# Gate scans in two halves of 64 rows, one of them amid the heads; weight rounding on GpSimd

## What is computed

```python
B, S, D, H = 16, 256, 256, 8
# x, ctx: (16, 256, 256)

def mlstm(q, k, v):                    # per batch; k = v = ctx
    ifg = jnp.concatenate([q, k, v], axis=-1)
    ig = (ifg @ igate_w.T + igate_b).T
    fg = (ifg @ fgate_w.T + fgate_b).T
    cs = jnp.cumsum(jax.nn.log_sigmoid(fg), axis=1)
    log_D = where(tril, cs[:, :, None] - cs[:, None, :], -inf) + ig[:, None, :]
    max_log_D = jnp.max(log_D, axis=-1, keepdims=True)
    C = einsum('hsd,htd->hst', qh, kh) / sqrt(32) * jnp.exp(log_D - max_log_D)
    norm = jnp.maximum(jnp.abs(C.sum(-1, keepdims=True)), jnp.exp(-max_log_D))
    h = einsum('hst,htd->hsd', C / (norm + EPS), vh)
    return layernorm(h) * ln_scale

def fake_quant_weight(w):              # 8 bits, one scale for the tensor
    scale = jnp.max(jnp.abs(w)) / 127
    return jnp.clip(jnp.round(w / scale), -128, 127) * scale

x = x + tanh(g_xattn[0]) * mlstm(layernorm(x), ctx, ctx)
x = x + tanh(g_ffn[0]) * lora_ffn(layernorm(x))     # both weights fake-quantised
x = x + tanh(g_xattn[1]) * attention(layernorm(x), ctx)
x = x + tanh(g_ffn[1]) * moe(layernorm(x))
return x
```

## Time and profile before

| | |
|---|---|
| median of three runs | 1244.83 us |
| the profiled execution | 1246.31 us, of which the span of its records 1244.7 us |
| TensorE busy | 1131.0 us (91%) |
| VectorE busy | 890.8 us (72%) |
| ScalarE busy | 699.2 us (56%) |
| GpSimd busy | 427.4 us (34%) |

### The profile page before, as it was taken

The page is one execution under the profiler, slowest core; times in us unless marked ns, Lnnn a source line. Parts: engine busy times, 40 slices in busy tenths (PEclk is TensorE's granted clock), DMA queues, the critical chain, the costliest instruction groups (busy, mean ns, idle before and its releaser), DMA issues. The chain is left out here.

```text
span 1244.7 us, 28091 instructions
## 1 busy us (share of the span) xinstructions
PE 1131.0 (91%) x9256; PEld 956.5 (77%) x9257; DVE 890.8 (72%) x2039; ACT 699.2 (56%) x1580; POOL 427.4 (34%) x559
## 2 busy tenths in 40 slices
PE   4958887999998799999999789889999999998997
PEld 1336565798987577777766489778999999997997
DVE  6739998667676788888887378457666767664656
ACT  1358875555563467676665544246655555553543
POOL 1237885713121110110130025664223333224563
PEclk9868989999998899999998978889999999998999
DMA  9245651100003564454452037658355454535564
GB/s 324 66 175 205 201 200 33 44 0 0 0 0 73 110 138 100 87 119 101 89 107 54 3 130 269 238 189 278 118 170 168 154 166 163 168 128 161 187 197 142
DMA packets 97181, 163.51 MB, mean 131 GB/s; under 512 B 12039, under 2 KB 71707, under 8 KB 94779
## 3 DMA queue, kind: packets, MB, share of 16 engines
q1 hardware_dynamic: 87067, 134.51, 37.2%
q0 software_dynamic: 9264, 27.01, 6.3%
q10 hardware_dynamic: 752, 0.73, 0.2%
HBM read 102.47 MB, written 33.69 MB: 109 GB/s over the span
## 5 line engine op out<-in xcount | busy, mean ns | idle before, releaser
L1677 DVE TENSOR_REDUCE c_mx<-c_s 128x2 f32<-128x512 f32 x256 | 164.4, 686 | 20.4 <-PE c_s L1823 20.1
L1598 ACT ACTIVATE c_probs<-c_t 128x512 f32<-128x512 f32 x256 | 139.0, 597 | 28.8 <-PE c_t L1846 27.9
L2773 ACT ACTIVATE d_g_full<-d_bank,d_e_bias 128x256 f32<-128x256 f32 x156 | 77.6, 497 | 108.6 <-PE d_bank L34 108.6
L32 PE MATMUL d_bank<-de_zt_hi,d_e_hi 128*128 128x256 f32 x312 | 91.1, 292 | 0.0
L34 PE MATMUL d_bank<-d_w_hi,d_g_lo 128*128 x312 | 88.0, 282 | 0.0
L33 PE MATMUL d_bank<-d_w_lo,d_g_hi 128*128 x312 | 88.0, 282 | 0.0
L34 PE MATMUL d_bank<-de_zt_hi,d_e_lo 128*128 128x256 f32 x312 | 87.8, 281 | 0.0
L32 PE MATMUL d_bank<-d_w_hi,d_g_hi 128*128 x312 | 87.8, 281 | 0.0
L33 PE MATMUL d_bank<-de_zt_lo,d_e_hi 128*128 128x256 f32 x312 | 87.6, 281 | 0.0
L2802 DVE TENSOR_TENSOR d_g_lo<-d_g_full,d_g_hi 128x256 fp32r<-128x256 f32 x156 | 65.9, 461 | 24.7 <-ACT d_g_hi L2774 24.7
L2933 POOL DMA_INDIRECT d_w_lo<-d_y_rows,d_pos x64 | 62.9, 983 | 56.4 <-ACT d_g_hi L2946 19.4
(11 more groups left out here) (413 smaller groups left out, 3814.2 us busy)
## 6 DMA issues: line engine op xcount, KB each, us to landing
d_e_raw<-in_w SPq DMA_DIRECT2D x39, 514.0 KB, 3.6
a_mb<-a_maxima SPq DMA_DIRECT2D x16, 1024.0 KB, 7.6
d_w_hi<-d_zt_kept SPq DMA_DIRECT2D x26, 512.0 KB
d_z_in<-d_z_rows POOLq DMA_DIRECT2D x39, 256.0 KB, 4.2
d_y_rows<-de_ys SPq DMA_DIRECT2D x39, 256.0 KB, 2.1
c_kt<-c_k_hi SPq DMA_DIRECT2D x64, 128.0 KB, 3.2
c_qt<-c_q_hi SPq DMA_DIRECT2D x64, 128.0 KB, 3.7
d_zt_kept<-d_w_hi SPq DMA_DIRECT2D x32, 256.0 KB
```

The source lines that it names most:

```text
L32: tensor.matmul(out, lhs_hi, rhs_hi, start=start, stop=False)
L1598: act.activation(probs[h % PR][:], t_ps[k][:], ACT.Exp).then_inc(exp_done, 1)
L1677: dve.tensor_reduce(mx[n % 2][:, :, k, p:p + 1], s_ps[h % SB][:], AX.X, ALU.max).then_inc(max_done, 1)
L2773: act.activation(g_full[:, m, :], hid[m][:, 0:TOK], ACT.Gelu, bias=bias[u][:, m:m + 1]).then_inc(gelu_full, 1)
```

## The change

The rows of gates are treated in two halves of 64 rows (batches 0 to 7 and 8 to 15), by a class `GateRows` whose tiles live on through the heads' stage.

- First half: in the gates' loop. `sizes(0)` is at VectorE's i = 6, Exp and Ln are on ScalarE behind step 5, `scans(0)` is at VectorE's i = 7 ahead of norm(7), the threshold on ScalarE behind step 6, and the transposes on TensorE ahead of query(7). SP stores its maxima behind the rows of step 6, and loads batch 0's once the rows of step 7 are issued.
- Second half: amid the heads. `sizes(1)` is in batch 0 and `scans(1)` in batch 1 on VectorE, each behind the first two products; Exp and Ln are on ScalarE behind the decays of batch 0, the threshold behind those of batch 1; the transposes are in batch 2 on TensorE, which then waits for VectorE's copy. SP stores its maxima ahead of its load of mb for batch 3.
- The two weights are rounded by GpSimd, one of the three passes behind each of `rstds(2)` to `rstds(7)`.
- In the heads' stage GpSimd's masks(0) stands ahead of the two memsets of va.

The diff, cut to its core:

```diff
+class GateRows:
+    HALVES = 2
+    LAST = 2
...
+        self.last_rows = sb("last_rows", [Mlstm.ROWS, self.LAST * S])
+        self.placed = [sem(f"placed{k}") for k in range(3)]
...
+    def wait_placed(self, engine, k):
+        steps = ((4,), (3, 1))[k]
+        for i, n in enumerate(steps):
+            engine.wait_ge(self.placed[k + i], 64 * n)
+    def sizes(self, dve, k):
+        self.wait_placed(dve, k)
+        f = self.part(self.f, k)
+        dve.scalar_tensor_tensor(out=self.part(self.size, k), in0=f, scalar=-1.0, in1=f, op0=ALU.mult, op1=ALU.max).then_inc(self.size_done, 1)
+    def logarithms(self, act, k):
+        small = self.part(self.small, k)
+        act.wait_ge(self.size_done, k + 1)
+        act.activation(small, self.part(self.size, k), ACT.Exp, scale=-1.0).then_inc(self.exp_done, 1)
+        act.wait_ge(self.exp_done, k + 1)
+        act.activation(small, small, ACT.Ln, bias=1.0).then_inc(self.ln_done, 1)
+    def scans(self, dve, k):
+        step = Chain(dve, self.scan, 2)
+        step.begin(k)
+        f, small, log_f = self.part(self.f, k), self.part(self.small, k), self.part(self.size, k)
+        cs, a, m = self.part(self.cs, k), self.part(self.a, k), self.part(self.m, k)
+        dve.wait_ge(self.ln_done, k + 1)
+        dve.wait_ge(self.zero_set, 1)
+        step(dve.scalar_tensor_tensor(out=log_f, in0=f, scalar=0.0, in1=small, op0=ALU.min, op1=ALU.subtract))
+        step(dve.tensor_tensor_scan(cs, log_f, self.part(self.zero, k), 0.0, ALU.add, ALU.add))
+        dve.tensor_tensor(a, self.part(self.gate_i, k), cs, ALU.subtract).then_inc(self.a_done, 1)
+        dve.wait_ge(self.a_done, k + 1)
+        dve.tensor_tensor_scan(m, a, a, -3e38, ALU.max, ALU.max).then_inc(self.m_done, 1)
+        dve.wait_ge(self.m_done, k + 1)
+        dve.scalar_tensor_tensor(out=small, in0=cs, scalar=-1.0, in1=m, op0=ALU.mult, op1=ALU.subtract).then_inc(self.max_done, 1)
+    def thresholds(self, act, k):
+        act.wait_ge(self.max_done, k + 1)
+        act.activation(self.part(self.thr, k), self.part(self.small, k), ACT.Exp).then_inc(self.thr_done, 1)
+    def turn(self, pe, k, out):
+        corner = self.ident[self.N * k:self.N * (k + 1), self.N * k:self.N * (k + 1)]
+        for i, (rows, done) in enumerate(((self.a, self.a_done), (self.thr, self.thr_done))):
+            pe.wait_ge(done, k + 1)
+            for j in range(Mlstm.J):
+                mm = pe.transpose(out[:, i, j, :], self.part(rows, k)[:, j * P:(j + 1) * P], corner)
+        mm.then_inc(self.turned, 1)
+    def keep_turned(self, dve, k, out):
+        dve.wait_ge(self.turned, k + 1)
+        dve.tensor_copy(self.tok_all[:, :, :, self.N * k:self.N * (k + 1)], out).then_inc(self.tok_done, 1)
+    def keep_maxima(self, sync, k):
+        b = Mlstm.B // self.HALVES
+        sync.wait_ge(self.m_done, k + 1)
+        sync.dma_start(self.m_dram[b * k:b * (k + 1)].rearrange("b h s -> (b h) s"), self.part(self.m, k)).then_inc(self.m_kept[k], 16)
...
+        SCANNED, PLACED = STEPS // 2, STEPS - 1
+        def gate_rows(n, some):
+            return g_rows[some, n * TOK:(n + 1) * TOK] if n < PLACED else rows.last_rows[some, :]
         def place_rows(queue, n, at, dst):
...
+            placed = rows.placed[0 if n < SCANNED else 1 if n < PLACED else 2]
+            for b in range(2):
+                row = H * (2 * n + b)
+                queue.dma_start(dst[row:row + H, :], gate_rows(n, slice(at, at + H))[:, b * S:(b + 1) * S]).then_inc(placed, 16)
...
+                place_rows(sync, n, 0, rows.f)
+                if n < PLACED:
+                    place_rows(sync, n, LO, rows.gate_i)
+                if n == STEPS - 2:
+                    rows.keep_maxima(sync, 0)
+            sync.wait_ge(rows.m_kept[0], 16)
             first.load_maxima(sync)
-            sync.wait_ge(m_kept, 16)
+            for k in range(2):
+                sync.wait_ge(rows.placed[k], 64 * (SCANNED, PLACED - SCANNED)[k])
...
+            def quantise(i, part):
+                flat = w_raw[i][:]
+                kept = lora.w1[:].rearrange("p a b -> p (a b)") if i == 0 else lora.w2[:, :, 0:D]
+                if part == 0:
+                    pool.wait_ge(inverted, i + 1)
+                    pool.tensor_scalar(flat, flat, inv[:, i:i + 1], ROUND, ALU.mult, ALU.add).then_inc(scaled_w, 1)
+                if part == 1:
+                    pool.wait_ge(scaled_w, i + 1)
+                    pool.tensor_scalar(flat, flat, -ROUND, QMAX, ALU.add, ALU.min).then_inc(bounded, 1)
+                if part == 2:
+                    pool.wait_ge(bounded, i + 1)
+                    pool.tensor_scalar(kept, flat if i == 0 else flat.rearrange("p (a b) -> p a b", a=lora.KF), -QMAX - 1.0, None,
+                                       ALU.max).then_inc(rounded, 1)
             for n in range(STEPS):
                 rstds(n)
-            pool.wait_ge(built, 3)
+                if 2 <= n < 5:
+                    quantise(0, n - 2)
+                if n >= 5:
+                    quantise(1, n - 5)
...
                 if n in (4, 6):
                     raise_hi(0 if n == 4 else 1)
+                if n == 5:
+                    rows.logarithms(act, 0)
+                if n == 6:
+                    rows.thresholds(act, 0)
             act.wait_ge(rows_done, STEPS)
-            place_rows(act, STEPS - 1, LO, gate_i)
...
+            place_rows(act, STEPS - 1, LO, rows.gate_i)
...
-            def quantise(i):
...
                     largest(0)
                 if i == 2:
                     scales(0)
-                    quantise(0)
                 if i == 3:
                     split_down()
                 if i == 4:
...
                 if i == 5:
                     scales(1)
                     scale_by_tanh()
+                if i == 6:
+                    rows.sizes(dve, 0)
+                if i == 7:
+                    rows.scans(dve, 0)
                 if i == STEPS:
-                    quantise(1)
                     raise_lo(0)
                     raise_lo(1)
...
+                    rows.keep_turned(dve, 0, tok_ps[:])
+            dve.wait_ge(rows.tok_done, 1)
...
                 if n in (1, 4):
                     turn_amax(0 if n == 1 else 1)
                 turn(n)
+            rows.turn(pe, 0, tok_ps)
             query_part(STEPS - 1)
...
+        tok_ps = hvt[0][:, S:2 * S].rearrange("p (k j r) -> p k j r", k=2, j=J)
...
                 u = n % R
                 after(sync, decay_done, 2 * (n + 1 - MR) * H)
+                if n == 3:
+                    rows.keep_maxima(sync, 1)
+                if n == B // 2:
+                    sync.wait_ge(rows.m_kept[1], 16)
                 sync.dma_start(mb[n % MR][:], m_dram[n].partition_broadcast(P)).then_inc(m_loaded[n % MR], 16)
...
+            masks(0)
             for i in range(R):
                 pool.memset(va[i][:], 0.0).then_inc(built, 1)
-            masks(0)
             pool.wait_ge(built, R)
...
             for n in range(B):
                 act.wait_ge(masked, 2 * (n + 1))
+                if n == B // 2:
+                    act.wait_ge(rows.tok_done, 2)
                 for h in range(H):
                     decays(n, h)
...
                         keep_outputs(n - 1, 3)
+                if n == 0:
+                    rows.logarithms(act, 1)
+                if n == 1:
+                    rows.thresholds(act, 1)
             for g in range(GROUPS):
...
             for n in range(B):
                 for h in range(0, QUAD, PAIR):
                     weigh(n, h)
+                if n == 0:
+                    rows.sizes(dve, 1)
+                if n == 1:
+                    rows.scans(dve, 1)
                 if n >= 2:
                     h_stat(n - 2)
...
                     h_norm(n - 2)
+                if n == 2:
+                    rows.keep_turned(dve, 1, tok_ps)
                 if n >= 1:
                     normalise(n - 1)
...
                 scores(n, 1)
                 if n > 0:
                     turn_outputs(n - 1)
+                if n == 2:
+                    rows.turn(pe, 1, tok_ps)
+                    pe.wait_ge(rows.tok_done, 2)
                 if n == 0:
                     pe.wait_ge(built, 2 * R)
```

84 lines of the change are left out of this document (27 added, 57 removed).

## The result

The changed kernel takes 1257.8 us (median of four runs, 1254.0 to 1259.1) beside 1244.2 us of the kernel before (median of four), a ratio of 1.0088 with a 95% interval of 1.0061 to 1.0115: 0.9% slower (the two medians themselves lie 1.1% apart, inside that interval). Forecast were 1239.4 us and faster, in a range of 1234 to 1246. The profiled execution took 1259.1 us and its records span 1257.3; before's span 1244.7. The loss is 12.6 us in this pair of traces, and it stands in two places: the gates' stage with its GpSimd passes, and the heads.

What follows compares the result with a forecast made beforehand. It saw TensorE's 4.58 us beat and stall in the gates' loop, a serial tail, and later heads bound by VectorE. Gain of 8.55 at the maxima load less 3.1 in the heads gave -5.45 us: 1239.4, range 1234 to 1246.

Steps and rivals of the forecast that it cites:

- The price of a GpSimd pass: Gates' loop: a rounding pass over 2048 columns on GpSimd takes 2.15 us, between bounds of 2.1 and 4.7.
- The collision: Gates' loop: VectorE operations with two SBUF inputs wait for GpSimd; split_down's subtraction takes back about 2 us, leaving 3.7.
- It hides under 3.2 us a pass: Gates' loop: GpSimd's rstd of 1.4 us plus a pass fits TensorE's beat of 4.58, up to about 3.2 a pass.
- Rival C: Gates' stage: GpSimd becomes the bound, maxima load at 40.6 + 6q for q us a pass, kernel slower; chance 0.10.
- what leaves VectorE: Gates' loop: without rounding, step 2 turns near 28.5 at full clock; about 5.8 us gained without the collision.
- the tail: Behind the gates' loop: query(7)'s end to the load of the maxima takes 2.05 us instead of 9.99.
- Its landing: Start of the heads: batch 0's maxima, loaded at 63.7, let the first mask start at 68.7 instead of 77.22.
- ScalarE's insertion in the heads: After batch 0's decays: Exp, load, Ln and load add 3.45 us on ScalarE.
- The heads: Heads' stage: the second half's work costs 3.1 us, 6.5 if the maxima land late, no less than 1.
- The maxima of batch 3: Heads: their load, alone in the queue, takes 5 us; masks of batch 3 come at 100.2 to 102.4.
- The sum: Whole kernel: -8.55 at the load of the maxima and +3.1 in the heads give -5.45 us.

Runs made afterwards that it cites:

- The probe: The kernel before plus fourteen GpSimd passes over 2048 columns behind the gates' stage, seven alone and seven beside VectorE operations; 1278.5 us including the added work.
- changed_again: The changed kernel itself, run again on a second chip beside the kernel before; ratio 1.0086 (1.0054 to 1.0118).
- two_fast_passes: The changed kernel with two GpSimd passes a weight (multiply-add, then add and multiply by 1.0), clip left out; 0.9965 of the kernel before.
- fast_passes_heads_reordered: The changed kernel with two fast GpSimd passes, second maxima's store moved to batch 6 and transposed half's copy ahead of h_norm; 0.9985 of the kernel before.
- two_fast_passes_scans_whole: The kernel before with rounding on GpSimd in two fast passes a weight, clip left out, scans whole behind the loop; ratio 0.9990 (0.9971 to 1.0009).

## Why the prediction was wrong

By the steps of the prediction:

- **The price of a GpSimd pass failed.** "A pass has one tensor input, like the cast: I take 2.15." The bounds were 2.1 and 4.7, and the passes took 1.98, 7.16, 5.38 and 1.98, 7.17, 5.80, which is 4.91 in the mean. The cast at 1.04 us for 1024 columns shares the one tensor input but not the pair of operations. No row of before had a tensor_scalar of that width on GpSimd; I bounded it by rows of other operations and then took the lower end, and the upper bound, for all its distance, lay below two of the three passes of each weight. The Trainium skill, "GPSIMD Engine Reference", section "Engine selection", calls one-input work there roughly line rate. The runs contradict that for five of the seven passes priced alone.
- **The collision failed, in whom it holds.** I counted only "a VectorE operation with two SBUF inputs". The probe has tensor_scalar and copy from SBUF held longer (5.02 and 4.95 us) than subtraction and scan (3.43 and 3.69). The norm, the cast, the copy and the small tensor_scalar of the loop were therefore not free; the subtraction of split_down, the one that I had named, ran free at 28.93 (0.21 us), and the cast behind it was held. The Trainium skill, "SBUF — State Buffer", section "Who interferes with whom", has copy, cast and tensor_scalar among those that can take the shared ports, and tensor_reduce not. The probe agrees on copy, tensor_scalar and tensor_reduce, the changed kernel's trace on the cast. I had used one half of that section, the half that my row showed. The section's words on a lock for the whole instruction, which the prediction puts to two inputs from SBUF, stand there with the two-port modes of the first three; that is also how the runs have it, since the operations with two inputs were let go 1.2 to 1.5 us before the pass ended.
- **"It hides under 3.2 us a pass" failed with them,** and not only by the size. It asked whether GpSimd has room in a beat of 4.58. It had: its rstd was never waited for. The other question, what stands still on VectorE while the pass runs, has the pass's whole length for an answer whenever VectorE comes to one held operation. Of the five holds, that of the cast made TensorE wait 6.62 us and that of the norm 3.76, and behind both it ran at half clock.
- **Rival C had the sign and the place, but too little.** Its formula, 40.6 + 6q, gives 70.1 at the measured mean of 4.91; the load was at 78.1. It put six passes and five rstds back to back. In the trace GpSimd stands idle 2.62, 0.74, 2.02 us for statistics that VectorE reached late, behind the held cast, copy and tensor_scalar: the engines took turns, and each one's delay came back to the other. Its chance of 0.10 rested on the row of the cast.
- **Right: what leaves VectorE.** Turn of step 2 at 28.5 and full clock; it was 28.85 and 1.09 us. One slip in the working behind it: 6.2 less 0.8 is 5.4, not 5.8.
- **Right: the tail.** From query(7) to the load 2.05 forecast, 2.09 measured. (Its landing wasn't: 5.9 us to the first mask instead of 4.95, and 5.2 to 5.9 in all nine traces with halves beside 4.8 to 5.0 in before and the three others with whole scans; no run shows why.) ScalarE's insertion in the heads 3.45, measured 3.46 (91.88 to 95.34), with two table loads of 1.28 us as the row of before had it. The Trainium skill, "ScalarE: Activation LUTs", has both functions in one set (section "Table sets: the hidden batching unit") and 2.66 us a switch (section "What ACT_TABLE_LOAD costs"); neither came true here.
- **The heads: right in mechanism, but their term was too small.** Batches 1, 2, 3, 4, 5 against batch 0 were forecast +0.5, +3.3, +5.6, +3.9, +3.1 and came +0.9, +3.8, +7.8, +6.0, +5.2. The maxima of batch 3 landed in 5.4 us (forecast 5). What was missed is TensorE's clock, for which the working of the heads has no term: it was at half in part of batch 1 and of batch 2. In `changed_again`, where it was full in batch 2, the same batches came +0.9, +4.5, +6.1, +4.4, +3.5, and from batch 0 to 15 the heads took 2.5 us more than before's in its first trace, against my 3.1. In the trace of the result it was 6.9 us; of these, 1.7 arise behind batch 5, where I had expected no more, and no run explains them.
- **The sum with its two failed terms mended.** `two_fast_passes` has passes near 2 us and the halves, though two passes a weight instead of three: -4.4 us by its ratio (-1.7 to -6.8) where the sum had -5.45. Its parts are further off than its sum: 6.1 us earlier at the load instead of 8.55, and 1.6 us longer in the heads instead of 3.1. So the rest of the working stands within what was measured, in part because two misses run against each other.

From the forecast's -5.45 us to the +12.6 of the traces it is 18.1 us: 14.4 at the load (78.11 instead of 63.7), 1.0 at its landing, 3.8 in the heads, less the 1.1 behind. The first term is the passes and what they held, by the runs above.

## What to carry to other kernels

Work moved to an engine that "has time" is priced by two questions: how long is one of its instructions, for exactly this pair of operations, and which operations of the neighbour stand still as long as it runs. If the neighbour is the engine on the path, the length of the longest single instruction counts more than the sum: cut it into pieces, or find a form that is fast (here add with a multiplication by 1.0, 1.95 us instead of 5.4). And a halved tail is only a gain if the other half lands where its engines have room: here the heads took back 4.6 of 4.9 us in one pair of kernels and 1.1 of 5.1 in the other, by one trace each.

The best kernel of those run is `two_fast_passes`, 0.9965 (0.9945 to 0.9986). The two with two passes on VectorE, 0.9977 and 0.9978, can't be told from it, and neither can `fast_passes_heads_reordered` and `two_fast_passes_scans_whole`.

## What the runs showed of the hardware that I had not expected

- GpSimd's tensor_scalar over 2048 f32 columns: 1.97 us for multiply-add, 1.90 for add-multiply, 5.36 for max, min or add alone, 7.12 for add-min. A second operation that does nothing (times 1.0) makes the pass 2.8 times as fast.
- A VectorE copy, cast or tensor_scalar from SBUF that started beside a GpSimd pass ended with it (5.02, 4.95 and 3.35 us), even one of 48 columns (7.08 us). With two SBUF inputs VectorE was let go 1.2 to 1.5 us earlier (3.43, 3.68 and 3.69 us). With an input from PSUM, or as statistics or maximum, it wasn't held (0.42 and 0.43 us).
- Between GpSimd instructions that follow each other closely VectorE did get its turn: beside eight of about 1.1 us two casts took 0.38 and 0.22 us. The cut cost 1.9 us of GpSimd on 7.16.
